# The last three expert blocks of a mixture of experts: added to the tokens by TensorE instead of scattered

## The reference

```python
def _L1_ffn_ref(hidden_states, gate_w, expert_bias, shared_gate_w, shared_up_w, shared_down_w,
                experts_gate_up, experts_down):
    x = hidden_states.reshape(-1, h)
    scores = jax.nn.sigmoid(x @ gate_w)
    _, selected = jax.lax.top_k(scores + expert_bias[None, :], K)        # K = 2
    top_scores = jnp.take_along_axis(scores, selected, axis=1)
    top_scores = top_scores / (top_scores.sum(-1, keepdims=True) + 1e-20)
    shared = jax.nn.silu(x @ shared_gate_w) * (x @ shared_up_w) @ shared_down_w
    comb = jnp.zeros((T, E), jnp.float32).at[jnp.arange(T)[:, None], selected].add(top_scores)
    for e in range(E):                                                   # E = 16
        gu = x @ experts_gate_up[e]
        g, u = jnp.split(gu, 2, axis=-1)
        routed = routed + comb[:, e:e + 1] * (jax.nn.silu(g) * u @ experts_down[e])
    return (shared + routed).reshape(b, s, h)
...
x = x + jnp.tanh(g_ffn[1]) * _L1_ffn_ref(_layernorm(x, axis=-1), ...)
```

## Time and profile before

| | us |
|---|---|
| median of 3 runs | 541.28 |
| the profiled execution | 541.45 |
| its span, first to last instruction | 539.6 |
| PE busy in the span | 496.2 (92%) |
| DVE busy | 411.0 (76%) |
| ACT busy | 313.5 (58%) |
| POOL busy | 286.3 (53%) |

### The profile page before, as it was taken

One profiled execution on the slowest core, in us unless ns is written; L12 is line 12 of the kernel. 1 busy time (PEld: TensorE's weight loads), 2 busy tenths in 40 slices (PEclk: granted clock), 3 DMA queues, 4 the chain that ended last, 5 costly groups with the idle time before them and its releaser, 6 DMA issues.

```text
span 539.6 us, 9216 instructions
## 1 busy us (share of the span) xinstructions
PE 496.2 (92%) x2799; PEld 383.8 (71%) x2799; DVE 411.0 (76%) x1049; ACT 313.5 (58%) x799; POOL 286.3 (53%) x295
## 2 busy tenths in 40 slices
PE   6977999989988998989999999999989977989986
PEld 3755688777867886557777777777766665777864
DVE  5998899974677758988999999999988764743322
ACT  4753654335544653477777777787767852155541
POOL 0060457657435745767687878786640036245560
PEclk9997999999999999999999999999999977999997
DMA  7596322223512419890918182725007402343426
GB/s 255 199 297 215 128 58 89 87 60 89 157 60 61 112 39 235 150 197 17 189 32 176 53 155 64 148 74 93 1 2 304 177 29 82 95 116 109 134 57 234
DMA packets 40442, 65.17 MB, mean 121 GB/s; under 512 B 4355, under 2 KB 30797, under 8 KB 40144
## 3 DMA queue, kind: packets, MB, share of 16 engines
q1 hardware_dynamic: 38144, 60.44, 41.1%
q0 software_dynamic: 2256, 4.21, 2.4%
HBM read 38.61 MB, written 27.99 MB: 123 GB/s over the span
## 4 chain that ended last, share of the span: by engine, by line
PE 61%; DVE 24%; DMA 5%; ACT 4%; issue 3%; POOL 1%; another core or an unknown queue 1%; SPq 1%; POOLq 0%; DVEq 0%
PE bank L1612 11%; PE bank L804 8%; PE bank L1667 5%; PE bank L1686 5%; PE bank L1656 5%; PE bank L1008 4%; PE bank L839 4%; PE bank L1629 3%; DVE left L2024 3%; PE bank L1646 3%; PE bank L1647 2%; PE bank L1633 2%; DVE best L2020 2%; PE bank L1024 2%; DVE hid L760 2%
## 5 line engine op out<-in xcount | busy, mean ns | idle before, releaser
L2143 DVE TENSOR_TENSOR qr<-bank,sinq 64x512 f32<-64x512 f32 x94 | 64.8, 689 | 2.1
L1427 POOL TENSOR_TENSOR qr<-qr 128x512 f32<-128x512 f32 x48 | 61.6, 1285 | 4.0 <-DVE qr L2143 3.5
L1853 ACT ACTIVATE silu<-bank,negm 128x256 f32<-128x256 f32 x128 | 59.2, 470 | 6.2 <-DVE negm L2157 6.0
L721 POOL TENSOR_TENSOR ffn_w_l<-ffn_raw,ffn_w_h 128x512 fp32r<-128x512 f32 x30 | 39.4, 1314 | 29.5 <-ACT ffn_w_h L733 29.4
L1432 POOL TENSOR_TENSOR hid<-silu,rden 128x256 f32<-128x256 f32 x55 | 33.8, 614 | 35.4 <-DVE rden L2162 35.2
L2157 DVE TENSOR_REDUCE negm<-bank 128x2 f32<-128x512 f32 x64 | 44.2, 691 | 6.7 <-PE bank L1647 3.7
L745 ACT ACTIVATE hid_h<-hid 128x512 fp32r<-128x512 f32 x28 | 17.7, 631 | 51.8 <-DVE hid L760 45.5
L1860 ACT ACTIVATE hid<-silu,rden 128x256 f32<-128x256 f32 x55 | 27.9, 507 | 34.0 <-DVE rden L2162 34.0
L963 POOL DMA_INDIRECT y_rows<-moe_y,route_rows x31 | 30.1, 972 | 32.4 <-issue 16.6
L804 PE MATMUL bank<-xT_h,ffn_w_h 128*128 128x512 f32 x120 | 40.2, 417 | 3.9 <-DVE xT_l L416 3.9
L1866 ACT ACTIVATE probsT<-bank 128x512 f32<-128x512 f32 x64 | 37.8, 591 | 9.7 <-PE bank L1656 9.5
(11 more groups left out here) (263 smaller groups left out, 1413.9 us busy)
## 6 DMA issues: line engine op xcount, KB each, us to landing
xn_slots<-blank SPq DMA_DIRECT2D x8, 2056.0 KB, 13.0
ffn_raw<-in_w_ffn SPq DMA_DIRECT2D x30, 256.0 KB, 2.7
pair_w<-in_pair_w SPq DMA_DIRECT2D x8, 768.0 KB, 5.3
moe_w<-in_w_moe SPq DMA_DIRECT2D x1, 6144.0 KB, 18.2
moe_x<-xn_slots SPq DMA_DIRECT2D x31, 128.5 KB
ffn_raw<-in_w_ffn SPq DMA_DIRECT2D x30, 128.0 KB, 2.3
folds<-att_w_raw SPq DMA_DIRECT2D x6, 640.0 KB, 7.3
att_w_raw<-folds SPq DMA_DIRECT2D x6, 384.0 KB, 12.7
```

The source lines that it names most:

```text
L721: nc.gpsimd.tensor_tensor(wt_l[b][:, 0:GU], raw[b][:, 0:GU], wt_h[b][:, 0:GU], ALU.subtract).then_inc(self.wgl, 1)
L1427: nc.gpsimd.tensor_tensor(qr[n][:, 0, :], qr[n][:, 0, :], qr[n][:, 1, :], ALU.add).then_inc(s_turned, 1)
L1853: last = nc.scalar.activation(ex[u % 2][:, h, :], bank[4 + u % 2][:, h * S:(h + 1) * S], ACT.Exp, bias=negm[:, u % 2, h:h + 1], accum_out= ...
L2143: last = nc.vector.tensor_tensor(by_sin[other, :, :], q2[hs, :, :], sinq[hs, j:j + 1, :].broadcast_to([C, 2, S]), ALU.mult)
```

## The change

The last three blocks (`LAST = 3`, so blocks 28, 29 and 30; `NSC = 28` blocks are still scattered) no longer go through `y_rows`. ACT writes each block's result times its routing weight as a high part in fp32r, DVE the rest as a low part. Three zero-one matrices of 128 rows x 1024 tokens say which token each row belongs to, and PE multiplies them into the banks of all eight token tiles: 16 products of 256 columns a block. For that, SP fetches the row numbers of these blocks in step 8 and writes the routing weights to DRAM, DVE works out the tokens in step 12 and makes the matrices in steps 13 to 18, and POOL gathers the weights after scatters 13, 16 and 19. Since some rows of `y_rows` are no longer written, all of them are cleared to zero in the attention, along with 128 spare rows of `xn_slots`; the token numbers are loaded there too. DVE adds the banks of the even tiles to `x` before its multiply-adds. The ten products with zeros go.

```diff
+LAST = 3
+NSC = NBLK - LAST
...
             def prog_pool(self, pool):
                 self.place(pool, 0)
                 self.place(pool, 1)
-                for b in range(NBLK):
+                for b in range(NSC):
                     self.scatter(pool, b)
+                    if b in GATHER_AT:
+                        self.gather(pool, GATHER_AT.index(b))
...
+            def last_rows(self, sp):
+                sp.wait_ge(s_diag, 1)
+                sp.dma_start(weight_of.rearrange("(p n) d -> p (n d)", p=P),
+                             wts[:].rearrange("p t j -> p (t j)")).then_inc(s_cell, 16)
+                first = self.values(mybir.EngineType.SP, row_at, NSC, E1 * T)
+                for k in range(LAST):
+                    sp.dma_start(last_row[:, k, :], xn2[bass.ds(first[NSC + k], P), XW - 16:XW]).then_inc(s_cell, 16)
...
+                if b - 2 >= NSC:
+                    pe.wait_ge(s_diag, HOTS + b - 2 - NSC + 1)
                 nc.tensor.matmul(bank[6 + b % 2][:, 0:D], hmT[b % 2][:], cells[:, bass.ds(cell + GU, D)],
...
+                    if b == NBLK - 1:
+                        self.odd_tiles(0)
                     if 1 <= b <= NBLK:
                         self.turn_hidden(pe, b - 1)
+                    if b == NBLK + 1:
+                        self.last_block(pe, 0)
                     if b >= 2:
                         self.down(pe, b - 2, cell[b - 2])
+                    if b == NBLK:
+                        self.odd_tiles(2)
...
+                if b >= NSC:
+                    k = b - NSC
+                    act.wait_ge(s_xsc[0], 16 * (4 + LAST))
+                    nc.scalar.activation(last_h[k], bank[6 + b % 2][:, 0:D], ACT.Copy,
+                                         scale=last_weight[:, k:k + 1]).then_inc(s_my, 1)
+                    return
...
+            def last_tokens(self, dve, seq):
+                dve.wait_ge(s_cell, 16 * (2 + LAST))
+                seq.did(nc.vector.memset(last_weight[:], 0.0))
+                seq.link(nc.vector.tensor_copy(last_u[:], last_row[:, :, 15]))
+                nc.vector.tensor_scalar(last_i[:], last_u[:].bitcast(I32), 1, None,
+                                        ALU.logical_shift_right).then_inc(s_diag, 1)
+                dve.wait_ge(s_diag, TOKENS)
+                seq.link(nc.vector.tensor_copy(last_token[:], last_i[:]))
+
+            def one_hot(self, dve, k, j):
+                nc.vector.tensor_scalar(hot[k][:, cols], token[:, cols], last_token[:, k:k + 1], None,
+                                        ALU.is_equal).then_inc(s_diag, 1)
+
+            def last_low(self, dve, k):
+                dve.wait_ge(s_my, b + 1)
+                nc.vector.scalar_tensor_tensor(out=last_l[k], in0=bank[6 + b % 2][:, 0:D], scalar=last_weight[:, k:k + 1],
+                                               in1=last_h[k], op0=ALU.mult, op1=ALU.subtract).then_inc(s_diag, 1)
...
             def combine(self, dve, seq):
+                for t in range(0, NT, 2):
+                    dve.wait_ge(s_odd, t // 4 + 1)
+                    seq.did(nc.vector.tensor_tensor(x[:, t, :], self.sum_of(t), x[:, t, :], ALU.add))
+                seq.wait()
...
+            def last_block(self, pe, k):
+                for t in (*range(0, NT, 2), *range(1, NT, 2)):
+                    for part in (last_h, last_l):
+                        last = nc.tensor.matmul(self.sum_of(t), hot[k][:, t * P:(t + 1) * P], part[k],
...
             def combine_pe(self, pe):
-                for g in range(NT // 2):
-                    nc.tensor.matmul(bank[g][:, 0:D], ident[:], x[:, 2 * g + 1, :], start=True, stop=False,
-                                     skip_group_check=True)
-                pe.wait_ge(s_diag, NT)
-                for i in range(NYB):
-                    pe.wait_ge(s_ysc[i], 16 * len(range(i, NBLK, NYB)))
-                for _ in range(LAST_FILLS):
-                    nc.tensor.matmul(bank[5][:], zero[:, 0:P], zero[:], start=True, stop=True)
+                for k in range(1, LAST):
+                    self.last_block(pe, k)
...
             def finish_sp(self, sp):
                 for i in range(NYB):
-                    sp.wait_ge(s_ysc[i], 16 * len(range(i, NBLK, NYB)))
+                    sp.wait_ge(s_ysc[i], 16 * len(range(i, NSC, NYB)))
...
+                sp.dma_start(y2.rearrange("(p n) d -> p n d", p=P),
+                             blank[:, 0:D].unsqueeze(1).broadcast_to([P, 2 * T // P, D])).then_inc(s_clr, 16)
+                sp.dma_start(xn2[E1 * T:E1 * T + P], blank[:]).then_inc(s_clr, 16)
+                sp.dma_start(token[:], a["token"].partition_broadcast(P)).then_inc(s_cst, 16)
                 sp.wait_ge(s_rp, NPAIR * 2 * JT)
```

More of the change, by code:

```diff
@@ L213, in build @@
             diag = lsb("weight_diag", [P, NT, P])
-        xn2 = nc.dram_tensor("xn_slots", (E1 * T, XW), F32, kind="Internal").ap()
+            last_row = lsb("last_row", [P, LAST, 16])
+            last_u = lsb("last_row_at", [P, LAST], U32)
+            last_i = lsb("last_token_at", [P, LAST], I32)
+            last_token = lsb("last_token", [P, LAST])
+            last_weight = lsb("last_weight", [P, LAST])
+            token = rows
+            hot = [xT_h[:, 0, :], xT_h[:, 1, :], xT_l[:, 0, :]]
+            last_h = [hid_h[k // 2][:, k % 2 * D:(k % 2 + 1) * D] for k in range(LAST)]
+            last_l = [hid_l[k // 2][:, k % 2 * D:(k % 2 + 1) * D] for k in range(LAST)]
+        xn2 = nc.dram_tensor("xn_slots", (E1 * T + P, XW), F32, kind="Internal").ap()
         y2 = nc.dram_tensor("y_rows", (2 * T, D), F32, kind="Internal").ap()
+        weight_of = nc.dram_tensor("weight_of_row", (2 * T, 1), F32, kind="Internal").ap()
         folds = nc.dram_tensor("folds", (NPAIR, P, FW), F32, kind="Internal").ap()
@@ L239, in build @@
         s_gates = sem("gates_loaded")
-        s_diag, s_odd, s_odd_out = sems("result", "weight_diagonals", "odd_tile_summed", "odd_tile_out")
+        s_diag, s_odd, s_odd_out = sems("result", "weight_diagonals_and_last_blocks", "tiles_summed", "odd_tile_out")
         s_out = sem("out_stored")
@@ L984, in prog_sp @@
                     if b % 4 == 0:
-                        row.update(self.values(mybir.EngineType.SP, row_at, b, E1 * T - P))
+                        row.update(self.values(mybir.EngineType.SP, row_at, b, E1 * T))
                     if b == 0:
@@ L1052, in prog_pe, with odd_tiles @@
                         self.turn(pe, b + 2)
+            def odd_tiles(self, first):
+                for g in (first, first + 1):
+                    nc.tensor.matmul(bank[g][:, 0:D], ident[:], x[:, 2 * g + 1, :], start=True, stop=False,
+                                     skip_group_check=True)
             def act_turned(self, act, b):
@@ L1107, in prog_dve @@
                         self.hidden(dve, b)
+                    if b < NSC:
                         self.row(dve, b)
@@ L1110, in prog_dve @@
                         self.diagonal(dve, b - 4)
+                    if b == LAST_TOKENS_AT:
+                        self.last_tokens(dve, seq)
+                    if HOT_AT <= b < HOT_AT + 2 * LAST:
+                        self.one_hot(dve, (b - HOT_AT) // 2, (b - HOT_AT) % 2)
+                for k in range(LAST):
+                    self.last_low(dve, k)
             def diagonal(self, dve, n):
@@ L1125, in combine @@
                         op0=ALU.mult, op1=ALU.add).then_inc(s_fin, 1)
[L1127 to L1135 removed]
+            def last_block(self, pe, k):
+                pe.wait_ge(s_mhx, NBLK)
+                pe.wait_ge(s_diag, HOTS + k + 1)
+                for t in (*range(0, NT, 2), *range(1, NT, 2)):
+                    for part in (last_h, last_l):
+                        last = nc.tensor.matmul(self.sum_of(t), hot[k][:, t * P:(t + 1) * P], part[k],
+                                                start=(k == 0 and t % 4 == 0 and part is last_h),
+                                                stop=(k == LAST - 1 and t % 2 == 0 and part is last_l),
+                                                skip_group_check=True)
+                    if k == LAST - 1 and t % 4 == 2:
+                        last.then_inc(s_odd, 1)
+            def combine_pe(self, pe):
+                for k in range(1, LAST):
+                    self.last_block(pe, k)
                 for g in range(NT // 2):
@@ L2271, in _ @@
                 pick_weights(seq)
-                blocks.prog_dve(dve)
+                blocks.prog_dve(dve, seq)
                 dve.wait_ge(ffn1.acc, 2)
```

36 lines of the change are left out of this document (26 added, 10 removed).

## The result

The changed kernel took **544.18 us** (median of 16 runs, 541.9 to 546.5) beside 541.37 of the kernel before (16 runs, 540.33 to 542.65): ratio 1.0058, 95% interval 1.0043 to 1.0072, slower by 2.8 us where 3.0 faster was forecast. Later sets, each with both kernels on one chip, gave 0.995 on chip 13, 0.9957 and 0.9946 on chip 1, and 1.0047 on chip 8; the chip of the first measurement is not on record. So there are two results, and both needed an explanation.

A forecast was written before the change was run, and what follows sets the result against it. PE was taken to bound the block loop, and waits for scatters and result loads the stretch after it. 3.7 us gained at the end less 0.7 lost by sync gave 3.0 net: 538.3 us, range 537.3 to 539.2.

The forecast's parts named there:

- DVE and POOL inside the loop: Block loop: DVE's six comparisons and tiny steps and POOL's three 1.27 us gathers fit in idle time, cost 0.
- Rival 2: Block loop near 490.6 us: an unexplained 2.33 us step vanishes, gaining 0.8; time 537.5, chance 0.12.
- Sync's detour: Sync queue after block 8's load: store, register reads and small loads delay block 9's load 1.1 us; stall 0.7.
- Rival 1: Sync queue: its extra work costs 1.3 to 2.5 through small packets or register reads; time 538.9 to 540.1, chance 0.15.
- The end: After the loop: computation ends at 533.4 instead of 537.13, DVE last; gain 3.7 us, bounds 2.9 to 3.96.
- The four adds: DVE at the end: adds of bank and token for even tiles, 0.42 each, overlapped 0.38, from 528.0 to 529.6.
- The comparisons: DVE, one 128x512 comparison in each of six blocks: 0.5 to 0.8 us each, under 1.08 idle, cost 0.
- the clears: Attention: 2.6 MB more take 12 us, hidden under sync's wait of 46.6 us; cost 0.
- The sum: Whole kernel: 3.7 gained, 0.7 lost, 3.0 net; 538.3 us against the median.
- The chance of 0.07 for slower: Whole kernel: probability given to a slower result, beside 0.85 for faster (under 540.2 us) and 0.08 for same.

The follow-up runs named there:

- k: Changed kernel with each of DVE's six comparisons made twice, the extra one into a tile nobody reads: 537.17 us, 0.9938 of the kernel before, chip 1.
- f: Changed kernel with sync's register reads and small loads spread over blocks 3 to 6, weight store still behind block 8's load: 536.61 us, 0.9929 of the kernel before, chip 1.
- j: Changed kernel with sync's extra work spread over blocks 3 to 8, second run: 536.4 us, 0.9922 of the kernel before, chip 1.
- r: Changed kernel with sync's extra work spread over blocks 3 to 8, third run: 544.05 us, 1.0026 of the kernel before, chip 3.
- e: Changed kernel again, without edit, against the kernel before on chip 1: 537.86 us, ratio 0.9957.
- l: Changed kernel without the low parts of the last three blocks, 24 products instead of 48: 537.81 us, 0.9946 of the kernel before, chip 1.
- d: Changed kernel without its loop additions (sync's small loads and weight store, comparisons, gathers), new end and clears kept: 535.85 us, 0.9909 of the kernel before, chip 13.

## Why the prediction was wrong

**The step that failed** is in "DVE and POOL inside the loop": "POOL gets three gathers of 1.27: it has 0.36 us a block to spare ... so block 27's scatter is not late." All of this came true (block 27's scatter is on time, POOL 1.05 us a gather), and it priced the wrong thing: the time that POOL takes to issue, not what the gather does to others. That second cost was put at nothing, and no row of the kernel before could have given it, since the indirect DMAs of its loop are scatters alone. In the first measurement PE's completions come late around the first gather: gate-up 13 to 30 took 33.2 us against 28.9, a loss of 4.3. On chip 3, side by side, the gathers cost 5.6. So the cause is shown for chip 3, where the gathers were taken away. For the first measurement it is argued, from the same late completions and the same kind of traces.

**Rival 2 was read the wrong way round.** The 2.33 us step was in the profile before. I took it as something that the change might make vanish, and gave it 0.12 with a gain. It did shrink (the step at block 14 is 1.75 instead of 2.39 us), and the same kind of delay came back several times over further on. A delay of PE's completions that no engine explains was evidence that the loop is open to such delays, and part of the rival's chance belonged on the other side.

**Sync's detour was mis-sized**: 0.7 taken, 1.3 measured, at its upper bound (0.5 to 1.3). Ten of the eleven profiles that have the whole of it show 1.2 to 1.5, k shows 0.8, and it is absent in f, j and r. Rival 1, which had 1.3 to 2.5, so had this term nearly right; of its two reasons the register read has some part (0.67 us on the chain, 0.5 taken), the small packets hardly any. Block 9's load was reckoned at 481.0; it left at 482.26, which is 481.47 in the time of before, since the loop ran 0.79 late there (gate-up 7 at 481.48 instead of 480.69). Two pieces were missing: I let the store start at 477.98, when its diagonal was done, but it stands behind block 8's own load (0.24 later); and from the store to the first small load it is 1.24 us (479.01 to 480.25), not 0.9. From there to block 9's load the 2.1 was right (2.01). So the load is 1.64 us late, the slack took 0.34 of it, and 1.3 is left.

**The end was right.** 3.7 forecast; 3.5 measured, by the column "end" (mean 20.4 before, 16.9 after). Products 0.12 apart, DVE the last, 14.07 us forecast from the last gate-up and 14.32 measured. The four adds took 1.42, where 1.6 was forecast. Wrong was that the rows would be there 1 us ahead or more: they land 12.9 to 13.2 us after that gate-up (e, l), where 12.3 was worked out, and the landing is on the chain in four of the sixteen profiles with this end (d, e, f and l).

**The comparisons** cost nothing, as forecast, and no cost of **the clears** was found. **The sum** for kind A then is 3.5 less 1.3, so 2.2, and 2.6 to 2.8 were measured (537.4 to 537.9 against 540.2 to 540.5); 538.3 with its range would have held there, with the detour 0.6 dearer than forecast. For kind B it is 3.5 less 1.3 less 4.3 to 5.6, a loss of 2.1 to 3.4, and 2.5 to 2.8 was measured. The chance of 0.07 for slower had no place for a chip that answers the same program otherwise.

**Not settled**: why a gather of 128 four-byte reads delays PE's completions some us later, and only on kind B. The traces show the late completions and the order of events, not the cause; PE's printed ends are modelled, so it can't be told whether PE or its signal was late. A fetch of instructions it was not in the first measurement: from 499 to 506 us only the queue of the loads and POOL's queue carried packets. For these inputs the last three blocks hold no rows (the last scatter of the kernel before moved 0.00 MB, where a full block is 128 KB), so all gathers here had the indices of empty slots, and gathers for real rows were not measured. It isn't known either what makes a chip one of kind A or B. No run tried the weights fetched without an indirect DMA, which is the version that should gain on both kinds: o (neither gathers nor detour) was 0.9936 on chip 3 and d 0.9909 on chip 13.

## What to carry to other kernels

A small indirect DMA can have two prices: the time that its engine takes to issue it, and what it does to the others a few us later (here 0 on one kind of chip and 5.6 us for three on the other). The second isn't in the row of the issue; take the operation away on its own and look at the cadence of the bounding engine. An unexplained long step in the profile before is a warning that more may come, not a reserve to be gained, and a verdict of half a per cent from one chip is half a result: measure on two. And count a detour in a queue from issue to issue, with the waits between them, before calling slack enough.

## What was not expected of the hardware

The same program took 537.4 to 537.9 us on chips 13 and 1 and 544.2 to 546.1 in the two measurements on the other kind, 1.6% from end to end, while the kernel before moved by 0.6% only (540.2 to 543.6). Three gathers of 128 numbers cost 0 on one kind and 5.6 us on the other. Three small loads cost nothing next to them when each went behind a full one, and a store, a register read and three small loads in a row behind one cost 1.3 us.
